# A gated cross-attention and FFN block on one core: where the middle part of the FFN weights is copied, where SyncE's loads stand, and a new order of all steps

## The reference, cut to what matters

```python
# xattn: hidden = ctx (4,256,128), z = layernorm(x)
x  = in_proj(hidden)                      # 256 channels
x  = silu(causal_conv4(x) + conv_b)       # u
dt_low, B, C = split(x_proj(x))           # 8, 16, 16 rows
dt = softplus(dt_proj(dt_low) + dt_b);  A = -exp(A_log)
state = state * exp(dt*A) + (dt*u) * B    # 16 states per channel, over 256 tokens
y = (sum_n state*C + D*u) * silu(z)
x = x + tanh(g0) * y
# ffn: hidden 704
xq = quant8(layernorm(x));  x1, x3 = split(xq @ w13.T)
inner = rmsnorm(relu(x1)**2 * x3) * norm_w
x = x + tanh(g1) * (quant8(inner) @ w2.T)
```

## Time and profile before

| | |
|---|---|
| median of 3 runs | 192.87 us (191.39 to 194.37) |
| profiled execution, device time | 192.29 us |
| profiled execution, span | 190.5 us |
| TensorE busy | 176.2 us (92%) |
| VectorE busy | 164.3 us (86%) |
| ScalarE busy | 153.9 us (81%) |
| GpSimd busy | 122.5 us (64%) |
| mean granted TensorE clock | 0.982 |

### The profile page before, as it was taken

How to read it: one execution, slowest core, us unless ns; L and a number is a source line. 1 busy time by engine, 2 the same in 40 slices (tenths; PEclk the granted TensorE clock), 3 DMA queues, 4 the chain that set the end, 5 groups by cost and what they waited for, 6 DMA issues and landing times.

```text
span 190.5 us, 3413 instructions
## 1 busy us (share of the span) xinstructions
PE 176.2 (92%) x1106; PEld 140.8 (74%) x1106; DVE 164.3 (86%) x266; ACT 153.9 (81%) x389; POOL 122.5 (64%) x88
## 2 busy tenths in 40 slices
PE   2897899989999999989999899999899999999984
PEld 1655897769988988867898678857767668787763
DVE  0579989988999999998899998979999999998291
ACT  4377999969799989988899889988998885765650
POOL 3000189987289999928999498799993997330000
PEclk9999699979999999999999999999999999999999
DMA  2698953034893140348910042968204000001001
GB/s 64 158 382 312 389 138 130 0 3 108 277 371 132 68 155 3 7 97 233 379 68 0 2 10 42 322 215 255 83 0 141 0 0 0 3 2 57 28 31 55
DMA packets 27314, 22.47 MB, mean 118 GB/s; under 512 B 15152, under 2 KB 21024, under 8 KB 27296
## 3 DMA queue, kind: packets, MB, share of 16 engines
q1 hardware_dynamic: 27296, 22.25, 38.2%
HBM read 18.98 MB, written 3.27 MB: 117 GB/s over the span
## 4 chain that ended last, share of the span: by engine, by line
PE 52%; DVE 23%; DMA 11%; issue 8%; SPq 4%; ACT 1%; DVEq 0%
PE m_ps L1061 20%; PE y_ps L1085 9%; PE w_ps L1115 8%; DMA bd<-b_diag 4%; DMA b_diag<-low 4%; PE w_ps L1132 3%; DMA x<-in_x 3%; PE y_ps L979 3%; DVE gg L925 2%; DVE bd L823 2%; DVE gam L930 2%; PE w_ps L1123 2%; DVE hb L883 2%; DVE xstat L848 1%; DVE x L893 1%
## 5 line engine op out<-in xcount | busy, mean ns | idle before, releaser
L404 POOL TENSOR_TENSOR hb<-hb,cs 128x1024 f32<-128x1024 f32 x31 | 72.9, 2368 | 2.2 <-DVE hb L883 1.4
L883 DVE TENSOR_TENSOR_SCAN hb<-dA,m_ps 128x1024 f32<-128x1024 f32 x30 | 67.8, 2275 | 4.4 <-PE m_ps L1061 1.6
L1061 PE MATMUL m_ps<-bd,duT 128*128 128x256 f32 (+1 forms) x216 | 57.9, 413 | 1.5 <-issue 1.1
L674 ACT ACTIVATE dA<-dt,nega 128x255 f32<-128x255 f32 (+1 forms) x144 | 54.5, 460 | 0.0
L1061 PEld LDWEIGHTS m_ps<-bd,duT 128*128 128x128 f32 x216 | 40.1, 194 | 10.7 <-issue 4.1
L1085 PE MATMUL y_ps<-identf,hb 128*128 128x128 f32 x256 | 31.8, 273 | 0.1
L1085 PEld LDWEIGHTS y_ps<-identf,hb 128*128 128x128 f32 x256 | 29.1, 141 | 3.4 <-issue 1.7
L1115 PE MATMUL w_ps<-w13T,xqT 128*128 128x352 bf16 x192 | 30.6, 313 | 0.8 <-ACT xqT L711 0.7
L1115 PEld LDWEIGHTS w_ps<-w13T,xqT 128*128 128x128 bf16 x192 | 18.5, 98 | 11.1 <-ACT xqT L711 1.3
L1132 PE MATMUL w_ps<-w2T,iqT 128*128 128x256 bf16 x144 | 16.7, 273 | 0.6 <-DVE ctx_in L956 0.5
L419 POOL TENSOR_TENSOR gw<-gg,normw 128x704 f32<-128x704 f32 x7 | 12.2, 1737 | 7.3 <-DVE gg L925 7.3
(11 more groups left out here) (143 smaller groups left out, 276.1 us busy)
## 6 DMA issues: line engine op xcount, KB each, us to landing
cs<-c_rows SPq DMA_DIRECT2D x16, 512.0 KB, 6.9
bd<-b_diag SPq DMA_DIRECT2D x10, 512.0 KB, 7.4
b_diag<-zeros SPq DMA_DIRECT2D x1, 2048.0 KB, 12.1
gw<-in_L_ffn_w SPq DMA_DIRECT2D x1, 1408.0 KB, 9.1
x<-in_x SPq DMA_DIRECT2D x1, 1024.0 KB, 6.0
out<-ctx_in SPq DMA_DIRECT2D x8, 128.0 KB, 1.7
ru<-in_L_ffn_w SPq DMA_DIRECT2D x1, 704.0 KB, 10.2
bd<-b_rows SPq DMA_DIRECT2D x2, 256.0 KB, 3.8
```

The source lines that it names most:

```text
L404: E.tensor_tensor(h_g, h_g, cs[:, s0:s0 + sn, l0:l0 + ln], ALU.mult).then_inc(hc_end if (b, i, h) == OUT_END else hc_ok[h], 1)
L674: last = act_fn(dA_g[:, s, 1:ln], dt[:, p, h, l0 + 1:l0 + ln], ACT.Exp, scale=nega[:, h, s0 + s:s0 + s + 1])
L883: V.tensor_tensor_scan(hb[:, k % 3, h], dA[:, k % 2, h].rearrange("p n l -> p (n l)"), m_ps[:, h], 0.0, ALU.mult, ALU.add).then_inc(scan_o ...
L1061: last = T.matmul(m_q[:, :, c * P - l0:(c + 1) * P - l0], duT[:, p, c, h * P:(h + 1) * P], bd[:, (s0 + sn // 2 * q) // GN, c, n0:n0 + sn / ...
```

## The change

The `w_mid` steps are gone from ScalarE. GpSimd now copies the remainder to bfloat16 as the first instruction of `w_lo`, and waits for its own copy before it subtracts. `winT` is copied by VectorE instead of ScalarE. The two convolution loads are issued by ScalarE, ahead of its table load. All other loads but the first two, and the zeros, are steps of SyncE's list (`l_...`, `zero`). All five lists have a new order; the TensorE, GpSimd and remaining ScalarE and VectorE steps are the same ones. The lists are cut below to the parts that are spoken of, SyncE's is whole; cut too are the bodies of load steps that are moved unchanged.

```diff
 PLAN = {
     "pe": """
-        ctxT/0.0 winT/0.0 inproj/0.0 inproj/0.1 warm/0.0 ctxT/1.0 dtwT/0.0 xpwT/0.0 inproj/1.0 xdbl/0.0 dtproj/0.0
-        warm/0.1 w/0.0 w/0.1 dtproj/0.1 w/0.2 warm/0.2 warm/0.3 warm/0.4 ctxT/2.0 bT/0.0 w/0.3 warm/0.5 warm/0.6
-        duT/0.0 bT/0.1 mix0/0.0 inproj/2.0 xdbl/1.0 duT/0.1 warm/0.7 mix1/0.0 mix0/0.1 dtproj/1.0 ctxT/3.0 mix1/0.1
-        w/0.4 mix0/0.2 skip/0.0 szT/0.0 sum0/0.0 w/0.5 mix1/0.2 sum1/0.0 sum0/0.1 w/0.6 mix0/0.3 sum1/0.1 w/0.7
-        duT/1.0 mix1/0.3 sum0/0.2 mix0/1.0 mix1/1.0 sum1/0.2 mix0/1.1 sum0/0.3 sum1/0.3 mix1/1.1 inproj/3.0 mix0/1.2
-        w/0.8 xdbl/2.0 mix1/1.2 skip/1.0 szT/1.0 sum0/1.0 dtproj/2.0 sum1/1.0 sum0/1.1 mix0/1.3 mix1/1.3 sum1/1.1
...
+        ctxT/0.0 winT/0.0 inproj/0.0 inproj/0.1 warm/0.0 xpwT/0.0 warm/0.1 ctxT/1.0 dtwT/0.0 inproj/1.0 xdbl/0.0
+        warm/0.2 dtproj/0.0 warm/0.3 w/0.0 ctxT/2.0 dtproj/0.1 bT/0.0 w/0.1 warm/0.4 duT/0.0 inproj/2.0 w/0.2
+        mix0/0.0 duT/0.1 w/0.3 xdbl/1.0 mix1/0.0 ctxT/3.0 mix0/0.1 dtproj/1.0 bT/0.1 mix1/0.1 warm/0.5 w/0.4
+        mix0/0.2 w/0.5 warm/0.6 mix1/0.2 warm/0.7 w/0.6 mix0/0.3 w/0.7 skip/0.0 sum0/0.0 mix1/0.3 sum1/0.0 sum0/0.1
+        sum1/0.1 sum0/0.2 sum1/0.2 w/0.8 duT/1.0 mix0/1.0 mix1/1.0 sum0/0.3 szT/0.0 sum1/0.3 mix0/1.1 mix1/1.1
+        xdbl/2.0 skip/1.0 sum0/1.0 inproj/3.0 dtproj/2.0 mix0/1.2 mix1/1.2 sum1/1.0 szT/1.0 sum0/1.1 mix0/1.3
...
     """,
     "act": """
-        ctxT/0.0 winT/0.0 tap/0.0 tap/0.1 sigm0/0.0 ctxT/1.0 sigm0/0.1 sigm1/0.0 xpwT/0.0 sigm1/0.1 nega/0.0 tap/1.0
-        absx/0.0 ln1q/0.0 sigm0/1.0 w_hi/0.0 w_hi/0.1 xrs/0.0 absx/0.1 w_hi/0.2 ln1q/0.1 w_mid/0.0 zsig/0.0 w_hi/0.3
-        ctxT/2.0 sigm1/1.0 duT/0.0 w_mid/0.1 decay0/0.0 decay1/0.0 tap/2.0 duT/0.1 w_mid/0.2 decay0/0.1 w_mid/0.3
-        decay1/0.1 decay0/0.2 absx/1.0 ctxT/3.0 w_hi/0.4 decay1/0.2 ln1q/1.0 zsig/1.0 w_hi/0.5 w_mid/0.4 w_hi/0.6
-        sigm0/2.0 szT/0.0 decay0/0.3 decay1/0.3 w_mid/0.5 duT/1.0 decay0/1.0 w_hi/0.7 decay1/1.0 decay0/1.1
...
+        ctxT/0.0 tap/0.0 tap/0.1 sigm0/0.0 xpwT/0.0 sigm0/0.1 sigm1/0.0 ctxT/1.0 sigm1/0.1 tap/1.0 nega/0.0 xrs/0.0
+        absx/0.0 ln1q/0.0 sigm0/1.0 w_hi/0.0 ctxT/2.0 absx/0.1 sigm1/1.0 ln1q/0.1 w_hi/0.1 zsig/0.0 tap/2.0 duT/0.0
+        w_hi/0.2 decay0/0.0 duT/0.1 w_hi/0.3 decay1/0.0 decay0/0.1 decay1/0.1 ctxT/3.0 decay0/0.2 absx/1.0 ln1q/1.0
+        w_hi/0.4 w_hi/0.5 sigm0/2.0 decay1/0.2 zsig/1.0 decay0/0.3 decay1/0.3 w_hi/0.6 w_hi/0.7 decay0/1.0 duT/1.0
+        decay1/1.0 decay0/1.1 sigm1/2.0 szT/0.0 w_hi/0.8 decay1/1.1 zsig/2.0 center/0.0 decay0/1.2 tap/3.0 rs1/0.0
...
     """,
     "dve": """
-        conv/0.0 conv/0.1 clamp/0.0 clamp/0.1 dtwT/0.0 u/0.0 xstat/0.0 u/0.1 xstat/1.0 lowc/0.0 conv/1.0 xstat/2.0
-        xstat/3.0 w_res/0.0 gates/0.0 series/0.0 w_res/0.1 series/0.1 dt/0.0 clamp/1.0 w_res/0.2 bd/0.0 dt/0.1
-        w_res/0.3 bd/0.1 scan0/0.0 conv/2.0 lowc/1.0 scan1/0.0 scan0/0.1 scan1/0.1 scan0/0.2 w_res/0.4 series/1.0
-        cubic/1.0 dt/1.0 scan1/0.2 du/1.0 w_res/0.5 w_res/0.6 scan0/0.3 scan1/0.3 scan0/1.0 scan1/1.0 clamp/2.0
-        scan0/1.1 w_res/0.7 yz/0.0 scan1/1.1 x1/0.0 conv/3.0 w_res/0.8 lowc/2.0 scan0/1.2 scan1/1.2 absx1/0.0
-        quant1/0.0 series/2.0 clamp/3.0 cubic/2.0 dt/2.0 gate/0.0 scan0/1.3 gate/0.1 du/2.0 gate/0.2 scan1/1.3
-        scan0/2.0 absmax/0.0 gate/0.3 scan1/2.0 yz/1.0 absmax/0.1 x1/1.0 scan0/2.1 absx1/1.0 scale2/0.0 quant1/1.0
-        outscale/0.0 lowc/3.0 scan1/2.1 scan0/2.2 gate/1.0 series/3.0 quant2/0.0 scan1/2.2 dt/3.0 gate/1.1
-        quant2/0.1 scan0/2.3 scan1/2.3 gate/1.2 scan0/3.0 absmax/1.0 gate/1.3 scan1/3.0 yz/2.0 x1/2.0 final/0.0
...
-        gate/2.3 absmax/2.0 out1/3.3 absmax/2.1 scale2/2.0 outscale/2.0 gate/3.0 quant2/2.0 quant2/2.1 gate/3.1
-        yz/3.1 x1/3.1 final/1.0 absmax/3.0 final/1.1 scale2/3.0 outscale/3.0 absx1/3.1 quant2/3.0 quant1/3.1
-        final/2.0 gate/3.2 gate/3.3 gated/3.1 absmax/3.1 final/2.1 scale2/3.1 quant2/3.1 outscale/3.1 final/3.0
...
+        winT/0.0 conv/0.0 conv/0.1 clamp/0.0 xstat/0.0 xstat/1.0 clamp/0.1 xstat/2.0 u/0.0 u/0.1 xstat/3.0 lowc/0.0
+        dtwT/0.0 conv/1.0 gates/0.0 series/0.0 clamp/1.0 w_res/0.0 dt/0.0 bd/0.0 series/0.1 w_res/0.1 dt/0.1
+        conv/2.0 w_res/0.2 scan0/0.0 lowc/1.0 w_res/0.3 scan1/0.0 scan0/0.1 bd/0.1 scan1/0.1 scan0/0.2 scan1/0.2
+        w_res/0.4 series/1.0 w_res/0.5 cubic/1.0 scan0/0.3 dt/1.0 clamp/2.0 w_res/0.6 w_res/0.7 du/1.0 scan1/0.3
+        scan0/1.0 scan1/1.0 yz/0.0 w_res/0.8 x1/0.0 scan0/1.1 lowc/2.0 scan1/1.1 absx1/0.0 conv/3.0 scan0/1.2
+        quant1/0.0 series/2.0 cubic/2.0 dt/2.0 clamp/3.0 gate/0.0 scan1/1.2 gate/0.1 du/2.0 scan0/1.3 gate/0.2
+        scan1/1.3 gate/0.3 absmax/0.0 scan0/2.0 scan1/2.0 absmax/0.1 yz/1.0 x1/1.0 scan0/2.1 scale2/0.0 scan1/2.1
+        absx1/1.0 outscale/0.0 quant1/1.0 lowc/3.0 scan0/2.2 scan1/2.2 series/3.0 quant2/0.0 gate/1.0 dt/3.0
...
+        gate/2.3 scan1/3.3 absmax/2.0 final/1.0 absmax/2.1 scale2/2.0 quant2/2.0 out1/3.3 outscale/2.0 quant2/2.1
+        gate/3.0 gate/3.1 yz/3.1 x1/3.1 absmax/3.0 scale2/3.0 outscale/3.0 final/1.1 quant2/3.0 final/2.0 absx1/3.1
+        quant1/3.1 gate/3.2 gate/3.3 gated/3.1 absmax/3.1 scale2/3.1 final/2.1 quant2/3.1 outscale/3.1 final/3.0
...
     """,
     "pool": """
-        cubic/0.0 dtadd/0.0 cubic/0.1 w_lo/0.0 du/0.0 u/1.0 dtadd/0.1 sz/0.0 du/0.1 diag/0.0 w_lo/0.1 w_lo/0.2
-        out0/0.0 w_lo/0.3 out1/0.0 out0/0.1 out1/0.1 dtadd/1.0 w_lo/0.4 out0/0.2 out1/0.2 out0/0.3 w_lo/0.5 out1/0.3
-        out0/1.0 w_lo/0.6 sz/1.0 u/2.0 out1/1.0 w_lo/0.7 out0/1.1 out1/1.1 out0/1.2 w_lo/0.8 dtadd/2.0 out1/1.2
-        gated/0.0 out0/1.3 sz/2.0 out1/1.3 gated/0.1 out0/2.0 out1/2.0 u/3.0 sz/3.0 out0/2.1 out1/2.1 cubic/3.0
...
+        diag/0.0 cubic/0.0 dtadd/0.0 du/0.0 u/1.0 cubic/0.1 w_lo/0.0 dtadd/0.1 du/0.1 w_lo/0.1 sz/0.0 w_lo/0.2
+        out0/0.0 out1/0.0 out0/0.1 w_lo/0.3 out1/0.1 out0/0.2 w_lo/0.4 out1/0.2 dtadd/1.0 w_lo/0.5 sz/1.0 out0/0.3
+        out1/0.3 out0/1.0 u/2.0 w_lo/0.6 out1/1.0 w_lo/0.7 out0/1.1 out1/1.1 w_lo/0.8 dtadd/2.0 out0/1.2 gated/0.0
+        out1/1.2 out0/1.3 out1/1.3 gated/0.1 out0/2.0 u/3.0 out1/2.0 sz/2.0 out0/2.1 sz/3.0 out1/2.1 out0/2.2
...
     """,
     "sp": """
-        cput/0.0 cget/0.0 cget/0.1 bput/1.0 bget/1.0 cput/1.0 bget/1.1 cget/0.2 cget/0.3 bget/1.2 cget/1.0 cget/1.1
-        cget/1.2 cget/1.3 bget/1.3 bput/2.0 cput/2.0 bget/2.0 bget/2.1 cget/2.0 cget/2.1 bget/2.2 bget/2.3 cget/2.2
-        cput/3.0 bput/3.0 bget/3.0 cget/2.3 cget/3.0 bget/3.1 cget/3.1 mput/3.0 mget/3.1 bget/3.2 bget/3.3 cget/3.2
-        store/0.0 store/0.1 cget/3.3 store/1.0 store/1.1 store/2.0 store/2.1 store/3.0 store/3.1
+        l_x/0.0 l_xpw/0.0 l_ctx/0.0 l_alog/0.0 l_dtb/0.0 l_g/0.0 l_d/0.0 l_dtw/0.0 l_w13/0.0 cput/0.0 cget/0.0
+        cget/0.1 l_w2/0.0 cput/1.0 cget/0.2 l_nw/0.0 zero/0.0 cget/0.3 cget/1.0 cget/1.1 bput/1.0 bget/1.0 bget/1.1
+        bget/1.2 cget/1.2 cget/1.3 bget/1.3 cput/2.0 bput/2.0 bget/2.0 cget/2.0 cget/2.1 bget/2.1 cget/2.2 bget/2.2
+        bget/2.3 mput/3.0 cput/3.0 cget/2.3 bput/3.0 bget/3.0 bget/3.1 cget/3.0 bget/3.2 bget/3.3 mget/3.1 cget/3.1
+        cget/3.2 store/0.0 cget/3.3 store/0.1 store/1.0 store/1.1 store/2.0 store/2.1 store/3.0 store/3.1
     """,
...
 FILLS = {
-    "winT": [("winT", "act")], "xpwT": [("xpwT", "act")], "dtwT": [("dtwT", "dve")], "w": [("w_res", "dve")],
+    "winT": [("winT", "dve")], "xpwT": [("xpwT", "act")], "dtwT": [("dtwT", "dve")], "w": [("w_res", "dve")],
     "ctxT": [("ctxT", "act")], "inproj": [("conv", "dve")], "xdbl": [("lowc", "dve")], "dtproj": [("absx", "act")],
     "bT": [("bd", "dve")], "duT": [("duT", "act")],
     "szT": [("szT", "act")], "xqT": [("xqT", "act")], "up": [("relu", "act"), ("gate", "dve")],
@@ -375,6 +375,10 @@
             if b == BATCH - 1:
                 return bd[:, slots(b, i)[0]:slots(b, i)[-1] + 1, i // 2]
             return bd[:, i].rearrange("p c n l -> p (c n l)").rearrange("p (g n l) -> p g n l", g=1, n=GN)
+
+        def column(n):
+
+            return a["L0_xattn_" + n].rearrange("(h p) -> p h", p=P)
 
         def products(eng, E, name, b, i):
 
@@ -423,32 +427,9 @@
             ctx_v = a["ctx_1024"].rearrange("b (h p) d -> p (b h) d", p=P)
             x_v = a["x"].rearrange("b (h p) l -> p b h l", p=P)
             xp = a["L0_xattn_x_proj_w"]
-            def small(t, n):
-                with nc.allow_non_contiguous_dma("one column of channels per half"):
-                    return sp.dma_start(t[:, :], a["L0_xattn_" + n].rearrange("(h p) -> p h", p=P))
 
             sp.dma_start(ctx_in[:, 0:HALVES, :], ctx_v[:, 0:HALVES, :]).then_inc(l_ctx0, 16)
             sp.dma_start(win_in[:, :, :], a["L0_xattn_in_proj_w"].rearrange("(h p) d -> p h d", p=P)).then_inc(l_win, 16)
-            sp.dma_start(convw[:, :, :], a["L0_xattn_conv_w"].rearrange("(h p) o k -> p h (o k)", p=P)).then_inc(l_conv, 16)
-            small(convb, "conv_b").then_inc(l_conv, 16)
-            sp.wait_ge(pool_k, 2)
...
```

(34 more changed lines are left out.)

72 lines of the change are left out of this document (40 added, 32 removed).

## The result

The changed kernel took **197.64 us** (median; 196.41 to 199.07, 4 runs), the kernel before, beside it, 192.44: ratio **1.027, 95% interval 1.020 to 1.033**. In a second series on another occasion it took 196.03 (195.67 to 196.62, 6 runs), with the kernel before spread from 190.41 to 201.47: ratio 1.010 (1.005 to 1.015). So the change makes the kernel slower, by 1 to 3%, where -1.2% was forecast. The ratios leave disturbed runs out (in the second series 17 of the 23 of the kernel before, whose median was 194.62), so a ratio can differ from the quotient of the medians. The kernel before is restless, and I read variants of the changed kernel first against each other.

What follows compares the result with a forecast made beforehand. The prediction took TensorE (92% busy, 52% of the chain) as the bound, with all four engines nearly full from 60 to 81 us. Its terms, -1.3 + 0.5 - 0.9 + 0.8 - 1.0 = -1.9, gave 190.6 us, range 187.0 to 195.5.

Steps and rivals of the forecast that it cites:

- part 5: Batch 3's b exchange: fetches follow each other directly, the 1.19 us wait at mix0/3.0 goes; -1.0 us, bounds +1 and -2.
- Part 1: The beginning: less VectorE work before the first scan, scan0/0.0 at 30.8 instead of 32.08; -1.3 us, bounds 0 and -2.2.
- Part 2: Nine copies moved from ScalarE to GpSimd, 0.8 us each, sometimes hold VectorE up; +0.5 us, bounds 0 and 7.
- rival (b): The full middle, 60 to 81 us: GpSimd, given four more copies, becomes the bound; 193.6 us, chance 0.18.
- Part 3: Cold stretch, 33 to 60 us: idle transposes moved into TensorE's pauses against the lower clock; -0.9 us, bounds -1.6 and +1.
- Part 4: Batch 1's zeros and b exchange: bput/1.0 held on SP, mix0/1.0 waits 1.1 us; +0.8 us, bounds 0 and 8.
- rival (c): Batch 1: the zeros land late, bput/1.0 goes out 8 us late, mix0/1.0 starts 9 us late; 199 us, chance 0.12.

Runs made afterwards that it cites:

- experiment 7: Changed kernel with batch 1's and batch 3's exchanges put early, plus the nine w_mid copies given back to ScalarE: 194.61 us, ratio 1.016.
- both repairs: Changed kernel with batch 3's exchange put back and batch 1's put early on SP: 191.60 us, ratio 1.000.
- experiment 4: Kernel before with only the nine w_mid copies moved from ScalarE to GpSimd: 196.93 us, ratio 1.015 (0.996 to 1.033).
- experiment 9: Kernel before with lowc/3.0 alone moved behind scan1/2.1 on VectorE: 196.75 us, ratio 1.013.
- experiment 2: Changed kernel with batch 1's exchange put early on SP (zeros before cput/1.0, bput/1.0 right behind it, bget/1.0 and 1.1 ahead of cget/1.1): 194.24 us, ratio 1.013.
- experiment 1: Changed kernel with batch 3's exchange put back (lowc/3.0 before scan1/2.1, cget/2.3 before mput/3.0): 192.14 us, ratio 1.006.
- experiment 5: Changed kernel with lowc/3.0 alone moved back ahead of scan1/2.1 on VectorE: 193.24 us, ratio 1.010.
- experiment 6: Changed kernel with cget/2.3 alone moved back ahead of mput/3.0 on SP, run twice: 193.49 us, and 192.71 in the second series.
- experiment 3: Changed kernel with batch 3's exchange put back and batch 1's put early, the kernel called both repairs: 191.60 us, ratio 1.000.

## Why the prediction was wrong

The range ended at 195.5, and the sign was wrong. The step that failed is part 5, the b exchange of batch 3. By its own steps:

- **Part 1, -1.3: right, by its own terms.** 30.8 was forecast for scan0/0.0. Conv/1.0 started 0.7 us later (0.9 taken) and the stretch from there to the scan was 2.0 us shorter (2.2 taken). The second series' trace has 31.59. VectorE of the changed kernel, beside the earlier trace rows:

```profile
30.75 2.28 DVE L897 TENSOR_TENSOR_SCAN hb<-dA,m_ps 128x1024 f32<-128x1024 f32 x1
```

- **Part 2, +0.5: the way was right, its size in time is not shown.** The prediction's working has a slip: nine chances at 0.8 us, one in ten, are 0.7. The copy was dearer on paper than on the chip. Copies of 512 columns took 0.62 to 0.64 us on the mean in place of 0.8, of 384 columns 0.51:

```profile
L577 POOL CAST w13T<-gg 128x512 bf16<-128x512 f32 x4 | 2.6, 644 | 0.5 <-DVE gg L822 0.5
L577 POOL CAST w2T<-gg 128x512 bf16<-128x512 f32 x3 | 1.9, 617 | 0.0
L577 POOL CAST w13T<-gg 128x384 bf16<-128x384 f32 x2 | 1.0, 506 | 0.0
```

  The copies do hold VectorE, one input or not. The q step of 256 columns, in the changed kernel, beside a copy that ran from 25.84 to 26.45 us; then the same step of experiment 7, whose copies are on ScalarE:

```profile
26.03 0.70 DVE L854 SCALAR_TENSOR_TENSOR q<-rr,q 128x256 f32<-128x256 f32 x1 [0.34 <-POOL rr L412]
```

```profile
26.03 0.42 DVE L859 SCALAR_TENSOR_TENSOR q<-rr,q 128x256 f32<-128x256 f32 x1 [0.34 <-POOL rr L415]
```

  The Trainium skill (SBUF — State Buffer, Who interferes with whom) has a VectorE instruction with two SBUF inputs contend with a GpSimd instruction that reads SBUF; the trace agrees, by 0.3 us here. In busy time VectorE has 164.7 us with both repairs (164.2 in the changed kernel) and 163.2 in experiment 7, so 1 to 1.5 us more with the nine copies on GpSimd in the new order; in the old order, experiment 4, 167.1 against 164.3, spread over several steps (the two products du, for one, 2.3 us in place of 1.6). The scans kept theirs. What of this reaches the time is not shown: with both repairs the same copies are better on GpSimd than at experiment 7's places on ScalarE, so rival (b) has support in the old order only (experiment 4).
- **Part 3, -0.9: the cold stretch of the middle is gone, but its worth is not shown, and the lower clock came earlier instead.** The rows of 33 to 60 and 56 to 60 us:

```profile
33.00:60.00 27.00, 24.83 (x167) 22.00 (x166) 25.65 (x23) 23.10 (x54) 24.70 (x17) 1.00 0.68 206
...
56.00:60.00 4.00, 1.83 (x16) 1.57 (x15) 2.95 (x2) 4.00 (x11) 3.92 (x4) 1.00 0.83 235
```

  The clock was 0.94 from 33 to 60 us in the earlier trace rows. From 20 to 30 us, however, it was 0.66 where the kernel before had 0.84, and over the whole execution 0.972 against 0.982. Nor does the stretch belong to the old order: experiment 9, which differs from the kernel before only behind 100 us, has 1.00 from 33 to 60. That trace prices it. Scan0/0.3 starts at 53.78 there against 55.20, 1.4 us sooner, but scan0/1.0 at 59.64 against 59.88: only 0.2 us are left, the rest goes into a wait for ScalarE's decays. The -0.9 had no such loss in it.
- **Part 4, +0.8: right in kind, a little too small.** bput/1.0 was issued at 45.75 (45.8 forecast), where the earlier trace rows had 37.03. The chain to it runs through GpSimd's list, three of the copies in it (1.6 us together), to out1/0.1, for which cget/1.1 waits:

```profile
41.12 0.56 POOL w13T L577
...
42.88 2.38 POOL hb L408
45.34 0.32 SPq L483
45.75 0.38 SPq L457
```

  The scatter took 8.35 us, not the 6.9 of batch 3, so bget/1.0 went out at 54.55 and not 52.8; it landed after 4.96 (5.1 taken). SyncE's issues, then TensorE:

```profile
45.75 4.02 SPq L457 DMA_DIRECT2D b_diag<-low  x2
54.55 1.89 SPq L464 DMA_DIRECT2D bd<-b_diag  x3
```

```profile
59.64 2.61 PE L1075 MATMUL m_ps<-bd,duT 128*128 128x256 f32 x11 [2.17 <-DMA bd<-b_diag]
```

  That is 2.2 us where 1.1 was forecast, and TensorE is busy for 1.83 us of the 4 from 56 to 60. By the repair (experiment 2) it costs 1.4 us at scan0/1.0 and 1.1 at scan0/2.0. How much of that the copies make by holding up out1/0.1 was not tried: no run has this late exchange with the copies on ScalarE. The 8 to 9 us of rival (c) didn't come: the zeros landed after 9.7 us, before bput/1.0's turn.
- **Part 5, -1.0: this is the step that failed.** The text said that "the pair lands about 3 us sooner after the scatter and 2 us are given back: the wait goes". Three things were wrong in it.

  First, what precedes the scatter on SP was left out. The sum looked only at what follows it. Cget/2.3, which before went out behind bget/3.0, now stands behind mput/3.0 and so waits for lowc/3.0 like everything else, and goes out right ahead of the scatter. That costs 0.5 us of issue and, by the fourteen traces above, about 1.5 us of scatter. With lowc/3.0 1.7 us later, bput/3.0 is issued 2.5 us later, and its turn takes 8.6 us in place of 7.3.

  Second, the pair was to land 3 us sooner after the scatter, by a median of 5.1 us per fetch. TensorE's matmuls began 9.5 us after bget/3.0 was issued, where the kernel before took 9.9: 0.3 us sooner. The second fetch took 8.87; its own row in the old trace, 8.08 us, was the price to take, not the median over all of bd's.

  Third, the 1.19 us of the earlier trace rows is the idle time of the weight load, which overlaps the matmuls. The matmuls themselves stood for 0.36 us. Without any wait for bd the stretch from scan0/2.0 to scan0/3.0 takes 33.6 us, 0.2 less than before: the -1.0 was not there to be had.

  Together: 2.5 + 1.3 - 0.3 = 3.4 us later for TensorE's matmuls (129.93 against 126.49), and 1.0 for the clock behind the wait. Scan0/3.0 came 4.4 us late where it should have come early.

Sum: parts 1 to 4 were forecast at -0.9 together, and scan1/2.3 stood at -0.55. That this is near is in part luck, since parts 3 and 4 came about otherwise than told. Part 5 came to +4.9 in the profiled execution, and +4.8 is the whole loss. Shown by experiment: the exchange of batch 3 carries most of it (experiments 1, 5, 6), batch 1's about 1 us more (experiments 2, 3). Open: why the clock fell behind the wait in one trace of the changed kernel and not in the other; how much of batch 1's part the copies make; and why the kernel before runs from 190 to 201 us with one and the same order.

## What to carry to other kernels

When an order is rewritten, take each DMA chain on the path (product, write, scatter, fetch) from its first wait on, and list what now stands ahead of it on the queue: one read that had been harmless is caught behind a wait and leaves with the transfer that matters. Price a transfer by the row with the same company, not by the median of its tile. And a part of a change has no price of its own: the same nine copies on GpSimd lose about 2 us (by the trace) in one order and, beside one placement on ScalarE, win 1 to 3 in the other, and one late VectorE step hit a DMA in one order and TensorE in the other.

## What the runs showed of the hardware

- A GpSimd copy with one input, 128x512 f32 to bf16, took 0.62 to 0.64 us, half of the 1.17 of the two-input subtraction of the same size, and as much as ScalarE's 0.62.
- From the issue of a scatter of b in batch 3 to that of the fetch behind it 7.75 to 8.6 us passed where a 512 KB read was issued 0.5 us ahead of it (five traces), 6.4 to 7.3 us where none was (nine). In the chain the scatter took 6.0 us with cget/2.3 out before lowc/3.0, 6.9 in the kernel before, 8.2 with a 512 KB read issued just ahead of it and 8.35 in batch 1 among other reads.
- One VectorE step of two inputs, 128x512, took 0.67 us, and 1.47 where a GpSimd product ran beside it. One of 128x256 took 0.42, and 0.70 beside a one-input GpSimd copy.
- Behind a TensorE wait of 2.95 us the granted clock was 0.50 from 131 to 133 us, and two matmuls took 2.08 us in place of 1.12. Behind waits of 2.27 and 2.99 us, in two other traces, it stayed at 1.00.
